# A recurrent scan inside a feed-forward kernel: four stacked copies of the states (high and low part against A's high and low part) in one fp32r product of 32 columns per step

## The chip, the cores and the metric

The kernel runs on one core of a Trainium2 chip. The metric is the device time of one execution in microseconds (us). The engines are named as in the profile: PE (TensorE), DVE (VectorE), ACT (ScalarE), POOL (GpSimd) and SP (SyncE, which issues transfers). They run side by side and meet at semaphores; each works through its own list in order.

## The reference, cut to what matters

```python
x = x + 0.5 * ffn(layernorm(x))                 # front FFN, weights ternary
xB = einsum('bsd,dn->sbn', layernorm(x), B)     # B is 128 x 16
def step(h, xb_t):                              # 512 steps in order, 8 sequences, 16 states
    h = tanh(xb_t + h @ A.T)
    return (h, h)
_, hs = scan(step, 0, xB)
x = x + einsum('sbn,nd->bsd', hs, C) @ W_out.T + b_out
x = x + 0.5 * ffn(layernorm(x))                 # the same FFN again
# ffn: silu(x w1) * (x w2), gelu(. h1), gelu(. h2), . w3 ; widths 128, 512, 512, 512, 128
```

x is 8 x 512 x 128, all of it float32.

## The kernel before

**Tiles and turns.** The 4096 tokens are cut into 8 chunks of 512 columns. The FFN runs over each chunk twice, so there are 16 turns (g = 0 to 15), each of some 25 us. A turn of the PE program is layer 2 of g (four output tiles m, four k each), the first layer of g+1 (`layer1`, four m), layer 3 of g (four m) and layer 4 of g, interleaved. Every product is two fp32r matmuls of 512 columns (`y_hi`, then `y_lo`, both against `w_hi`, L243), because activations are kept as a high part and a rest. ACT makes tanh and gelu (L933, L951, L954), DVE and POOL make the products of the gate and the rests `y_lo` (L659, L669, L676, L686, L1162).

**The scan.** The 512 steps of a sequence are cut into 8 blocks of 64, all blocks at once. A first pass runs chunks 3 to 7 of every block from zero, a full pass of 8 chunks then starts from the ends that the first one found. That is 13 chunk passes of 8 steps. The first four are in the early turns g = 2 to 5 (`early_turn`), the fifth and one of the full pass in g = 6, one each in g = 7 and 8 (`middle_turn`), and the last five in g = 9 to 13 (`turn`). Turns 0, 1, 14 and 15 hold no step. At the end the starts and the ends are compared for equality of every value, and only where they differ does another round run.

**A step before.** States lie on 128 partitions (8 sequences x 16 states) and a step has 8 columns (the blocks). PE multiplies by `a_blk`, A eight times on the diagonal, in float32 (L375), on top of the inputs that one product with `ident` put into the bank `SC` (L371, once for a chunk); ACT takes the tanh into `h_all` (L970). PE's next step waits for ACT's `step_h`.

**Around it.** `x_times_b` (L359) makes the inputs for all sequences, `own_xb` on DVE picks each one's own (L728, L732). `spread_states` on DVE (L713) writes the states of a chunk to 512 columns, each sequence's rows kept by a mask, and `attention` (L381) multiplies that by C W_out in float32; DVE adds it to x as `lnin` (L721). `front_tokens` and `to_features("f", ...)` are the transposes (L262, L272) on both sides of the layer norm that feeds `layer1` of the next turn: DVE takes statistics and normalises (L619, L624, L647), POOL makes the inverse root (L1154, L1157), ACT copies `xn_hi` (L928), DVE makes `xn_lo` (L654). `middle_tokens` (L252) does the same for the norm ahead of the scan.

The order on every engine is the order in which its program is written. There is no scheduler.

## Time and profile before

| | us |
|---|---|
| median of three runs (lowest, highest) | 430.62 (430.44, 431.69) |
| the profiled execution, its own time | 430.41 |
| its span, from the first to the last instruction | 428.6 |
| PE busy | 401.9 (94%) |
| PE weight loads busy | 315.5 (74%) |
| DVE busy | 323.7 (76%) |
| ACT busy | 233.8 (55%) |
| POOL busy | 165.0 (38%) |

A matmul's time in the profile holds its way through the array, and the next one starts long before it ends. So what a matmul costs is read from the distance of two starts. Granted clock of PE over the span: 0.988, and 1.00 in every stretch of 30 us from 30 to 390.

### The profile page before, as it was taken

The numbers are of one execution on the slowest core, as the hardware profiler recorded it, in microseconds if no ns is written. First come the engines' busy times: TensorE is split into PE (matmuls) and PEld (weight loads), VectorE is DVE, ScalarE is ACT, GpSimd is POOL, SyncE is SP. The second block draws the span as 40 slices with busy tenths as digits, with TensorE's granted clock in tenths as the row PEclk, the third lists the DMA queues.
The fourth block names the chain that finished last, engine by engine and source line by source line (L and its number), as shares of the span: only waits on it lengthen the run. The fifth ranks groups of instructions, "written<-read, shape, count | busy, mean of one in ns | idle before, by whom it ended". The sixth has DMA issues, their size and how long they took to land.

```text
span 428.6 us, 6790 instructions
## 1 busy us (share of the span) xinstructions
PE 401.9 (94%) x1917; PEld 315.5 (74%) x1917; DVE 323.7 (76%) x686; ACT 233.8 (55%) x466; POOL 165.0 (38%) x150
## 2 busy tenths in 40 slices
PE   5978999999999999999999999999999999999981
PEld 3756777878878787887777878787877878777660
DVE  4768898998989899569767686949678695978511
ACT  3656464664646466454565546466464656646450
POOL 3435253454514345323434332435343343534120
PEclk9899999999999999999999999999999999999996
DMA  8900000000000000001001010000101000010001
GB/s 260 419 10 2 25 2 17 11 0 26 1 25 0 17 7 0 26 0 50 1 1 51 0 50 0 26 25 2 49 0 49 0 24 24 0 50 1 26 1 33
DMA packets 6079, 14.03 MB, mean 33 GB/s; under 512 B 1056, under 2 KB 1568, under 8 KB 5792
## 3 DMA queue, kind: packets, MB, share of 16 engines
q1 hardware_dynamic: 5040, 13.37, 8.2%
q10 hardware_dynamic: 1008, 0.29, 0.3%
q8 instruction: 14, 0.23, 0.2%
q14 instruction: 17, 0.14, 0.1%
HBM read 7.37 MB, written 2.10 MB: 22 GB/s over the span
## 4 chain that ended last, share of the span: by engine, by line
PE 60%; DVE 16%; issue 11%; ACT 6%; POOL 3%; DMA 1%; DVEq 0%; ACTq 0%; POOLq 0%
PE F L243 47%; PE FR L243 5%; DVE y L669 3%; DVE y_lo L686 3%; DVE u L659 3%; DVE h_wide L713 2%; ACT y_hi L954 2%; PE SC L375 2%; DVE y_hi L676 2%; POOL y_lo L1162 2%; PE MI L381 2%; DVE xnt_f L647 1%; PE MI L252 1%; ACT y L951 1%; ACT th L933 1%
## 5 line engine op out<-in xcount | busy, mean ns | idle before, releaser
L243 PE MATMUL F<-y_hi,w_hi 128*128 128x512 f32 x512 | 214.6, 419 | 8.9 <-DVE y_lo L686 5.0
L243 PE MATMUL F<-y_lo,w_hi 128*128 128x512 f32 x512 | 202.0, 394 | 0.0
L1162 POOL TENSOR_TENSOR y_lo<-y,y_hi 128x512 fp32r<-128x512 f32 x96 | 133.2, 1401 | 129.5 <-ACT y_hi L954 63.7
L951 ACT ACTIVATE y<-F,sc 128x512 f32<-128x512 f32 x112 | 77.1, 688 | 121.6 <-PE F L243 121.5
L243 PEld LDWEIGHTS F<-y_hi,w_hi 128*128 128x128 f32 x512 | 96.4, 188 | 35.7 <-issue 11.4
L243 PEld LDWEIGHTS F<-y_lo,w_hi 128*128 128x128 f32 x512 | 96.5, 189 | 19.7 <-issue 1.9
L686 DVE TENSOR_TENSOR y_lo<-y,y_hi 128x512 fp32r<-128x512 f32 x96 | 83.8, 883 | 33.7 <-ACT y_hi L954 32.4
L954 ACT ACTIVATE y_hi<-F,sc 128x512 fp32r<-128x512 f32 x112 | 76.7, 684 | 0.0
L933 ACT ACTIVATE th<-F,s1h 128x512 f32<-128x512 f32 x61 | 42.2, 691 | 22.2 <-PE F L243 19.2
L243 PE MATMUL F<-xn_hi,w_hi 128*128 128x512 f32 x119 | 50.1, 421 | 3.0 <-POOL w_lo L1202 1.7
L243 PE MATMUL F<-xn_lo,w_hi 128*128 128x512 f32 x119 | 46.9, 394 | 0.0
L669 DVE SCALAR_TENSOR_TENSOR y<-F,s12h,u 128x512 f32<-128x512 f32 x58 | 43.5, 749 | 3.9 <-DVE u L659 0.3
L659 DVE SCALAR_TENSOR_TENSOR u<-th,F 128x512 f32<-128x512 f32 x61 | 41.6, 681 | 6.3 <-ACT th L933 6.0
L375 PEld LDWEIGHTS SC<-h_all,a_blk 128*128 128x128 f32 x208 | 38.1, 189 | 8.1
L676 DVE CAST y_hi<-y 128x512 fp32r<-128x512 f32 x60 | 34.8, 579 | 2.1
L970 ACT ACTIVATE h_all<-SC 128x8 f32 (+1 forms) x104 | 18.3, 176 | 27.4 <-PE SC L375 27.4
L375 PE MATMUL SC<-h_all,a_blk 128*128 (+1 forms) x208 | 30.1, 217 | 0.0
L243 PEld LDWEIGHTS F<-xn_hi,w_hi 128*128 128x128 f32 x119 | 22.4, 188 | 9.0 <-issue 4.0
L1154 POOL TENSOR_TENSOR ve_f<-mv_f,epsc 128x4 f32<-128x4 f32 x16 | 3.2, 200 | 66.7 <-DVE mv_f L624 61.8
L243 PE MATMUL FR<-y_hi,w_hi 128*128 128x512 f32 x64 | 26.3, 412 | 0.6 <-DVE y L669 0.6
L243 PE MATMUL FR<-y_lo,w_hi 128*128 128x512 f32 x64 | 25.2, 394 | 0.0
L243 PEld LDWEIGHTS F<-xn_lo,w_hi 128*128 128x128 f32 x119 | 22.5, 189 | 3.5
(113 smaller groups left out, 341.5 us busy)
## 6 DMA issues: line engine op xcount, KB each, us to landing
x_all<-in_xT SPq DMA_DIRECT2D x1, 2048.0 KB, 16.2
x_all<-x1c SPq DMA_DIRECT2D x8, 256.0 KB, 2.4
x_all<-lnin SPq DMA_DIRECT2D x8, 256.0 KB, 2.3
out<-outb SPq DMA_DIRECT2D x8, 256.0 KB, 2.0
x_all<-in_xtok SPq DMA_DIRECT2D x1, 1536.0 KB, 12.1
w_raw<-in_h1T SPq DMA_DIRECT2D x2, 512.0 KB, 7.9
w_raw<-in_h2T SPq DMA_DIRECT2D x2, 512.0 KB, 9.7
x_all<-in_xtok SPq DMA_DIRECT2D x2, 256.0 KB, 4.8
```

The costliest lines, as they stand in the source:

```text
L243: mm = nc.tensor.matmul(out, wtile(w, layer, k, m), y, start=first and i == 0, stop=last and i == len(pairs) - 1)
L375: nc.tensor.matmul(SC[:, t * BLOCKS:(t + 1) * BLOCKS], a_blk[:, :], h_all[:, bass.ds(off, BLOCKS)], start=False, stop=t == CSTEPS - 1, ski ...
L381: mm = nc.tensor.matmul(MI[:, :], cw_rep[:, :], h_wide[:, :, :].rearrange("p b s -> p (b s)"), start=True, stop=True)
L659: nc.vector.scalar_tensor_tensor(out=u[:, m % 2, :], in0=th[:, m % 2, :], scalar=1.0, in1=l1_banks(g, m, late)[0][:, :], op0=ALU.add, op1= ...
L669: nc.vector.scalar_tensor_tensor(out=y1[:, m, :], in0=l1_banks(g, m, late)[1][:, :], scalar=s12h[:, m:m + 1], in1=u[:, m % 2, :], op0=ALU. ...
L676: nc.vector.tensor_copy(y1_hi[:, m, :], y1[:, m, :]).then_inc(y1_hi_r, 1)
L686: nc.vector.tensor_tensor(y_lo[:, k, :], y[:, k, :], y_hi[:, k, :].bitcast(F32), ALU.subtract).then_inc(out_sem, 1)
L933: nc.scalar.activation(th[:, m % 2, :], l1_banks(g, m, late)[0][:, :], ACT.Tanh, scale=s1h[:, m:m + 1]).then_inc(th_r, 1)
L951: nc.scalar.activation(y23[:, m, :], bankt[:, :], ACT.Gelu, scale=s)
L954: nc.scalar.activation(y_hi[:, m, :], bankt[:, :], ACT.Gelu, scale=s).then_inc(hi_r, 1)
L970: nc.scalar.activation(h_all[:, bass.ds(c * HCOLS + (t + 1) * BLOCKS, BLOCKS)], SC[:, t * BLOCKS:(t + 1) * BLOCKS], ACT.Tanh).then_inc(ste ...
L1162: pool.tensor_tensor(y_lo[:, k, :], y[:, k, :], y_hi[:, k, :].bitcast(F32), ALU.subtract).then_inc(out_sem, 1)
```

## The change

The states get four copies on the partitions: two halves of the sequences (`HALVES`) by two, and in each 32 rows two sets of 16. A step now has 32 columns (4 sequences x 8 blocks). Rows 0 to 63 of `h` hold the low part of the states and rows 64 to 127 the high part; the columns of `a_mix` hold A's high and low part. One fp32r product of 128 x 128 by 32 columns makes a step. ACT takes the tanh twice (into `h`, and for the lower 64 rows once more, unrounded, back into the unused half of the bank `SC`), and DVE subtracts (`scan_low`) before PE may go on. The inputs are no longer put in by a product with the identity: `x_times_b` writes them straight into `SC` for the first pass, ACT keeps a copy (`keep_xb`), and writes it back for later chunks (`inject`). The own-sequence pick and the spread are gone; `attention` is two fp32r products of 256 columns. At the start DVE makes the mixed weights (`mix_parts`). The orders of the turns change on PE, ACT and DVE.

```diff
             def x_times_b(c):
                 pe.wait_ge(xn2_r, c + 1)
-                for j in range(SEQS // PAIR):
-                    rows = slice(j * PAIR * STATES, (j + 1) * PAIR * STATES)
-                    mm = nc.tensor.matmul(MI[rows, 0:PAIR * HCOLS],
-                                          b_rep[:, :, :].rearrange("p b n -> p (b n)"),
-                                          xn2[:, j * PAIR * HCOLS:(j + 1) * PAIR * HCOLS], start=True, stop=True)
+                wait(pe, step_h, c * CSTEPS)
+                for j in range(2 * HALVES):
+                    half = j % HALVES
+                    mm = nc.tensor.matmul(SC[j * 2 * STATES:(j + 1) * 2 * STATES, 0:HCOLS], b_rep[:, :],
+                                          xn2[:, half * HCOLS:(half + 1) * HCOLS], start=True, stop=True)
                 mm.then_inc(xb_mm, 1)
...
-                    nc.tensor.matmul(SC[:, 0:HCOLS], ident[:, :], cols(xb_all, c, HCOLS), start=True, stop=False,
-                                     skip_group_check=True)
-                wait(pe, step_h, s)
-                off = c * HCOLS + t * BLOCKS
-                nc.tensor.matmul(SC[:, t * BLOCKS:(t + 1) * BLOCKS], a_blk[:, :], h_all[:, bass.ds(off, BLOCKS)],
-                                 start=False, stop=t == CSTEPS - 1, skip_group_check=True).then_inc(step_mm, 1)
+                    pe.wait_ge(sc_set, n + 1)
+                wait(pe, step_h, n * CSTEPS + t)
+                if t == 0:
+                    states = h_first[:, :] if isinstance(c, int) and c == 0 else h[:, span(CSTEPS - 1)]
+                else:
+                    states = h[:, span(t - 1)]
+                nc.tensor.matmul(SC[:, span(t)], a_mix[:, :], states, start=False, stop=True,
+                                 skip_group_check=True).then_inc(step_mm, 1)
             def attention(gb, c):
-                pe.wait_ge(spread, gb + 1)
+                pe.wait_ge(step_h, (gb + FIRST_PASS + 1) * CSTEPS)
                 wait(pe, x2_r, gb)
-                mm = nc.tensor.matmul(MI[:, :], cw_rep[:, :], h_wide[:, :, :].rearrange("p b s -> p (b s)"),
-                                      start=True, stop=True)
+                for half in range(HALVES):
+                    mm = nc.tensor.matmul(MI[:, half * HCOLS:(half + 1) * HCOLS], cw_mix[:, half, :], h[:, :],
+                                          start=True, stop=True)
                 mm.then_inc(att_mm, 1)
...
# ACT
-                nc.scalar.activation(h_all[:, bass.ds(c * HCOLS + (t + 1) * BLOCKS, BLOCKS)],
-                                     SC[:, t * BLOCKS:(t + 1) * BLOCKS], ACT.Tanh).then_inc(step_h, 1)
+                nc.scalar.activation(h[:, span(t)], SC[:, span(t)], ACT.Tanh)
+                nc.scalar.activation(SC[0:64, span(CSTEPS + t)], SC[0:64, span(t)], ACT.Tanh).then_inc(step_t, 1)
+            def keep_xb(c):
+                act.wait_ge(xb_mm, c + 1)
+                place = (c + FIRST) % CHUNKS if isinstance(c, int) else c + FIRST
+                nc.scalar.copy(cols(xb_all, place, HCOLS), SC[:, 0:HCOLS]).then_inc(sc_set, 1)
+            def inject(n, c):
+                act.wait_ge(step_h, n * CSTEPS)
+                nc.scalar.copy(SC[:, 0:HCOLS], cols(xb_all, c, HCOLS)).then_inc(sc_set, 1)
...
# DVE
+            def scan_low(n, t):
+                dve.wait_ge(step_t, n * CSTEPS + t + 1)
+                nc.vector.tensor_tensor(h[0:64, span(t)], SC[0:64, span(CSTEPS + t)], h[0:64, span(t)].bitcast(F32),
+                                        ALU.subtract).then_inc(step_h, 1)
...
+            def mix_parts():
+                dve.wait_ge(parts, 1)
+                dve.wait_ge(cw_ready, 2)
+                for i, raw in enumerate((a_raw, cw_rep)):
+                    nc.vector.tensor_tensor(part_lo[:, i, :], raw[:, :], part_hi[:, i, :].bitcast(F32), ALU.subtract).then_inc(parts, 1)
+                dve.wait_ge(ld_scan, 48)
+                for i in range(3):
+                    nc.vector.tensor_scalar(part_own[:, i, :], part_hi[:, min(i, 1), :].bitcast(F32), mask[:, 2 * i:2 * i + 1], None,
+                                            ALU.mult).then_inc(parts, 1)
+                dve.wait_ge(parts, 6)
+                for i, out in enumerate((a_mix[:, :], cw_mix[:, 0, :], cw_mix[:, 1, :])):
+                    nc.vector.scalar_tensor_tensor(out=out, in0=part_lo[:, min(i, 1), :], scalar=mask[:, 2 * i + 1:2 * i + 2],
+                                                   in1=part_own[:, i, :], op0=ALU.mult, op1=ALU.add).then_inc(mixed, 1)
```

The orders of the turns move at many places; three of them follow as the built programs have them.

DVE, early turn g = 2 (before, from the statistics of the middle norm, `st_m`, to the first product of the gate, `u`):

```order
L619 BN_STATS st_m<-MI 128x6 x4
L622 MEMSET spare 128x1
L624 BN_AGGR mv_m<-st_m 128x2 x4
L619 BN_STATS st_f<-x_all 128x6 x4
L622 MEMSET spare 128x1
L624 BN_AGGR mv_f<-st_f 128x2 x4
L647 TENSOR_SCALAR xnt_m<-MI,mv_m,rs_m 128x128 x4
L647 TENSOR_SCALAR xnt_f<-x_all,mv_f,rs_f 128x128 x4
L686 TENSOR_TENSOR y_lo<-y,y_hi 128x512 x2
L659 SCALAR_TENSOR_TENSOR u<-th,F 128x512
```

The same place after the change, from step 1's subtraction on (`h<-SC,h` is `scan_low`):

```order
L721 TENSOR_TENSOR h<-SC,h 64x32
L658 TENSOR_SCALAR xnt_m<-MI,mv_m,rs_m 128x128 x4
L658 TENSOR_SCALAR xnt_f<-x_all,mv_f,rs_f 128x128 x4
L721 TENSOR_TENSOR h<-SC,h 64x32
L697 TENSOR_TENSOR y_lo<-y,y_hi 128x512
L721 TENSOR_TENSOR h<-SC,h 64x32
L697 TENSOR_TENSOR y_lo<-y,y_hi 128x512
L670 SCALAR_TENSOR_TENSOR u<-th,F 128x512
L721 TENSOR_TENSOR h<-SC,h 64x32
L680 SCALAR_TENSOR_TENSOR y<-F,s12h,u 128x512
```

Eight such subtractions stand in the turn; that of step 2 stands behind both normalisations, that of step 4 between the gate's two products.

DVE, the loop of late turns g = 10 to 13, after the change (before, the same rows without L721, and with the statistics first):

```order
L721 TENSOR_TENSOR h<-SC,h 64x32
L647 REGISTER_ALU
L630 BN_STATS st_f<-FR 128x6 x4
L632 REGISTER_ALU
L633 MEMSET spare 128x1
L635 BN_AGGR mv_f<-st_f 128x2 x4
L720 REGISTER_ALU
L721 TENSOR_TENSOR h<-SC,h 64x32
L54 REGISTER_ALU
L658 TENSOR_SCALAR xnt_f<-FR,mv_f,rs_f 128x128 x4
L720 REGISTER_ALU
L721 TENSOR_TENSOR h<-SC,h 64x32
```

Step 0's subtraction stands ahead of the statistics, step 1's ahead of the normalisation and step 2's behind it. On PE, in `turn`, step 0 now stands ahead of layer 2's first tile, step t behind its tile t-1, and `front_tokens` inside the first tile:

```diff
-                if not last:
-                    front_tokens(g + 1)
-                layer2(g, 0, gen)
                 step(0)
+                layer2(g, 0, gen, lambda k: front_tokens(g + 1) if k == 1 and not last else None)
+                step(1)
                 layer2(g, 1, gen)
-                step(1)
+                step(2)
                 layer2(g, 2, gen)
-                step(2)
+                step(3)
                 if not last:
                     to_features("f", xnt_f, FR, g + 1)
                 layer2(g, 3, gen)
-                step(3)
+                step(4)
```

ACT, early turn g = 2, after the change, from the tanh of step 5 on (L1046 and L1047 are a step's two tanh, L1009 the gate's, L1027 and L1030 a gelu's two):

```order
L1046 ACTIVATE h<-SC 128x32
L1047 ACTIVATE SC<-SC 64x32
L1009 ACTIVATE th<-F,s1h 128x512
L1027 ACTIVATE y<-F,sc 128x512
L1030 ACTIVATE y_hi<-F,sc 128x512
L1046 ACTIVATE h<-SC 128x32
L1047 ACTIVATE SC<-SC 64x32
L1027 ACTIVATE y<-FR,sc 128x512
```

Each step's pair stands one gelu earlier than before, so ACT waits there for a PE step that is issued behind the tile whose gelu comes next.

## Rows read from the trace of the kernel before

**Rows 1.** The page, part 1.

```profile
PE 401.9 (94%) x1917; PEld 315.5 (74%) x1917; DVE 323.7 (76%) x686; ACT 233.8 (55%) x466; POOL 165.0 (38%) x150
```

**Rows 2.** Timeline of PE, a step between two tiles: start, us, instruction.

```profile
135.37 0.28 PE L375 MATMUL SC<-h_all,a_blk 128*128 x2
135.51 0.47 PE L243 MATMUL F<-xn_hi,w_hi 128*128 128x512 f32 x1
135.82 0.39 PE L243 MATMUL F<-xn_lo,w_hi 128*128 128x512 f32 x1
136.05 0.40 PE L243 MATMUL F<-xn_hi,w_hi 128*128 128x512 f32 x1
```

**Rows 3.** Timeline of ACT, the tanh of the step in rows 2.

```profile
135.78 0.18 ACT L970 ACTIVATE h_all<-SC 128x8 f32 x1 [1.07 <-PE SC L375]
```

**Rows 4.** Groups by line and shape: count, busy us, mean ns.

```profile
L713 DVE TENSOR_TENSOR h_wide<-h_all,mask 128x512 f32<-128x512 f32 x8 | 14.2, 1779 | 0.0
...
L624 DVE BATCH_NORM_AGGREGATE mv_f<-st_f 128x2 f32<-128x6 f32 x64 | 6.0, 156 | 0.7
```

**Rows 5.** Timeline of PE, x_times_b in an early turn.

```profile
143.23 0.39 PE L243 MATMUL F<-y_lo,w_hi 128*128 128x512 f32 x1
143.55 0.43 PE L359 MATMUL MI<-xn,b_rep 128*32 128x128 f32 x8
143.91 0.66 PE L272 MATMUL FR<-ident,xnt_f 128*128 128x128 f32 x4
```

**Rows 6.** Timeline of DVE, early turn g = 4.

```profile
124.95 0.89 DVE L619 BATCH_NORM_STATS2 st_m<-MI 128x6 f32<-128x128 f32 x4 [0.98 <-PE MI L252]
...
129.12 3.08 DVE L647 TENSOR_SCALAR xnt_f<-x_all,mv_f,rs_f 128x128 f32 x4
...
133.44 0.69 DVE L659 SCALAR_TENSOR_TENSOR u<-th,F 128x512 f32<-128x512 f32 x1
...
145.38 1.29 DVE L686 TENSOR_TENSOR y_lo<-y,y_hi 128x512 fp32r<-128x512 f32 x2
```

**Rows 7.** Timeline of PE, early turn g = 4.

```profile
121.95 0.49 PE L243 MATMUL F<-y_hi,w_hi 128*128 128x512 f32 x1
...
130.79 0.28 PE L375 MATMUL SC<-h_all,a_blk 128*128 x2
...
131.32 0.48 PE L243 MATMUL F<-xn_hi,w_hi 128*128 128x512 f32 x1
...
146.21 0.47 PE L243 MATMUL F<-y_hi,w_hi 128*128 128x512 f32 x1 [0.26 <-DVE y_lo L686]
```

**Rows 8.** Timeline of DVE, late turn g = 11.

```profile
303.58 0.88 DVE L619 BATCH_NORM_STATS2 st_f<-FR 128x6 f32<-128x128 f32 x4
...
306.45 1.37 DVE L647 TENSOR_SCALAR xnt_f<-FR,mv_f,rs_f 128x128 f32<-128x128 f32 x4 [1.57 <-POOL rs_f L1157]
```

**Rows 9.** Timeline of ACT, late turn g = 11.

```profile
308.61 0.69 ACT L951 ACTIVATE y<-F,sc 128x512 f32<-128x512 f32 x1 [0.74 <-PE F L243]
...
309.82 0.60 ACT L928 CAST xn_hi<-FR 128x512 fp32r<-128x512 f32 x1
```

**Rows 10.** Timeline of PE, late turn g = 11.

```profile
311.37 0.49 PE L243 MATMUL F<-xn_hi,w_hi 128*128 128x512 f32 x1 [0.28 <-DVE xn_lo L654]
...
323.30 0.39 PE L243 MATMUL F<-y_lo,w_hi 128*128 128x512 f32 x1
323.79 1.12 PE L381 MATMUL MI<-h_wide,cw_rep 128*128 128x512 f32 x2
...
324.99 0.40 PE L243 MATMUL F<-y_lo,w_hi 128*128 128x512 f32 x1
```

**Rows 11.** Timeline of DVE, end of late turn g = 11.

```profile
325.02 0.69 DVE L686 TENSOR_TENSOR y_lo<-y,y_hi 128x512 fp32r<-128x512 f32 x1
```

**Rows 12.** Timeline of DVE at the start.

```profile
27.66 0.15 DVE L857 TENSOR_SCALAR general<-F 1x1 int32<-1x1 f32 x1 [1.59 <-PE F L606]
```

**Rows 13.** Windows, turn g = 11: length, busy us (records) by engine, clock, DMA.

```profile
303.94:329.11 25.17, 24.79 (x117) 19.62 (x116) 19.27 (x36) 13.78 (x29) 9.46 (x8) 1.00 0.05 21
```

More of the change, by code:

```diff
@@ L741, in early_turn, with step @@
+            def early_turn(g, mid, scan):
+                def step(t):
+                    if scan is not None:
+                        scan_low(scan, t)
                 xn_low(g + 1)
+                step(0)
                 if mid is not None:
@@ L747, in early_turn @@
                 normalise("f", g + 2, cols(xt_all, g + 2), mv_f, rs_f, xnt_f)
+                step(2)
                 low(g, 1, y2_hi_r, y23, y2_hi, y2_lo, y2_lo_dve)
+                step(3)
                 low(g, 3, y2_hi_r, y23, y2_hi, y2_lo, y2_lo_dve)
[L750 to L751 removed]
+                gate(g + 1, 0)
+                step(4)
+                gated(g + 1, 0)
+                gate(g + 1, 1)
+                y1_high(g + 1, 0)
+                gated(g + 1, 1)
+                step(5)
+                y1_high(g + 1, 1)
+                layer1(g + 1, 2)
+                step(6)
                 low(g, 1, y3_hi_r, y23, y3_hi, y3_lo, y3_lo_dve)
+                step(7)
                 low(g, 2, y3_hi_r, y23, y3_hi, y3_lo, y3_lo_dve)
```

309 lines of the change are left out of this document (179 added, 130 removed).

## The prediction

> **What bounds the kernel now.** I read the page first: PE is busy for 94% of the span, the others for 76% and less [rows 1]. Then the timelines of PE, DVE and ACT over one early turn, one late turn and the start. PE's list is nearly gapless; two matmuls of 512 columns start 0.23 us apart [rows 2]. In the early turn g = 4 (some 25 us from the first product of layer 2 at 121.95) PE waits at one place that the rows name, layer 4's last k at 146.21, for a rest that DVE makes [rows 7]. But DVE is close behind: from the statistics at 124.95 it works almost without a pause to that rest at 145.38, through a normalisation of 3.08 us that is slow because POOL works beside it [rows 6]. In the late turn g = 11 (25.17 us [rows 13]) PE waits before `layer1` for `xn_lo` [rows 10], which hangs on ACT's list (gelu, gelu, then `xn_hi` at 309.82 [rows 9]), and before attention for the spread. So the kernel is bound by PE with two chains through ACT and DVE hard beside it. What PE saves counts only outside these chains.
>
> **What PE saves.** A step between two matmuls: 135.82 - 135.37 - 0.23 = 0.22 us [rows 2], for two weight loads and two tiny products (x2 in the row of one step). One fp32r product is one of each: 0.11 saved, 104 x 0.11 = 11.4 us. The identity product is of the same kind: 13 x 0.22 = 2.9. Attention: 324.99 - 323.30 - 2 x 0.23 = 1.22 us, of it a wait of 0.26 (323.79 against 323.53) [rows 10]; the work of 0.96 becomes 512 columns in two pieces, 0.25, so 0.7 saved and the wait gone, at most 8 x 0.97 = 7.8. `x_times_b` costs 143.91 - 143.23 - 0.23 = 0.45 [rows 5], and its columns double: between 0 and 0.45 more; I take 0.2, since its four products write different rows and eight records lie within 0.43 us: 8 x 0.2 = 1.6 lost. Together 20.5 us if no one else set the pace.
>
> The Trainium skill (TensorE: Matmul & The Clock Gate, section on LDWEIGHTS) gives a load as its columns over 1.2 GHz, an estimate of 107 ns for 128. The trace agrees (0.22 for two), and by that rule alone the steps would give back 104 x 0.107 = 11.1 us.
>
> **What a step's result now waits for.** Before: ACT's tanh starts 0.41 us after the step's first product, 0.30 after its second [rows 2, 3]. Afterwards PE may go on when the first tanh, the second, and DVE's subtraction are done. A small operation on DVE takes 0.16 us [rows 4]; I take 0.10 to 0.16 of DVE's list and 0.15 until PE starts. That alone is some 0.8 us, and steps are 2 us apart in early and late turns. What matters is where the subtraction stands on DVE, whose list is in order.
>
> The Trainium skill (VectorE: DVE Perf Modes, section on the TRN2 errata) says that each small operation pays a fixed cost; its PSUM form, 120 cycles plus the elements, gives an estimate of 0.16 us for 32 elements, 16.5 us of DVE's time for 104. The row agrees for the single one. By that rule the turns where DVE is full get longer whatever PE saves, which is the direction of my forecast.
>
> **Early turns (g = 2 to 5).** Times from the turn's first product. Step 2's subtraction stands behind both normalisations. They end at 129.12 + 3.08 - 121.95 = 10.25 [rows 6, 7]; PE's pieces ahead of the statistics (one step, the identity) shrink by 0.33, so 9.9. The subtraction ends at 10.0, PE's step 3 may start at 10.15. Before it started at 130.79 - 121.95 = 8.84 [rows 7], and PE would now be there at 8.3: a wait of 1.8 us. `layer1` starts at 10.15 + 0.4 (the transposes; 131.32 - 130.79 is 0.53 with the old step) = 10.55, before 9.37 [rows 7]: 1.2 later. Queued on ACT behind the tanh of step 3 is the last gelu of layer 2, then the gate's tanh. From there DVE's chain (gate at 133.44 to the rest at 145.38: 11.9 us [rows 6]) gets four subtractions, the first of which sits between the gate's two products and waits for a step that PE issues after `layer1`: +0.2 to 0.7 in all. PE gets 0.44 back from four steps, and `x_times_b` lies in the wait before layer 4. DVE's chain decides: 1.2 + 0.3 - 0.4 (gelus and rests whose waits for ACT fall away as layer 3 comes with less queued) = 1.1 us longer, between 0.3 and 2.0. Four turns: +4.4. `own_xb` goes, 0.9 us at the end of DVE's turn, but the next statistics wait for PE's transposes, not for DVE (idle 0.98 us before them [rows 6]).
>
> **Late turns (g = 9 to 13).** Take the end of layer 3 (323.30 [rows 10]) as 0. DVE's last rest starts at 1.72 (325.02 [rows 11]) whatever attention costs, and layer 4's last k needs it: 2.47. With attention short PE waits there for 0.5, so of attention's 0.97 only 0.4 is real. Step 1 waits for the subtraction of step 0 behind layer 4's output (0.25). The statistics start at about 5.6, the normalisation ends 306.45 + 1.37 - 303.58 = 4.24 later [rows 8], 9.85, and step 2's subtraction behind it; PE's step 3, there at 9.8, starts at 10.15. ACT now takes the tanh of step 3 ahead of the third gelu: 10.15 + 0.3, and that gelu at 10.6. From a gelu's start to `layer1` it is 311.37 - 308.61 = 2.76, less 0.06 for a tanh that moved [rows 9, 10]: 13.3. Before, it was 311.37 - 323.30 + 25.17 = 13.24 [rows 10, 13]. So everything that PE saved in the first half is gone; the second half keeps four steps, 0.44. I take 0.35 saved a turn, between 0 and 0.9: five turns, -1.75.
>
> **Middle turns (g = 6 to 8).** In g = 6 sixteen steps stand 4 matmuls apart (0.94 + 0.11 = 1.05 us) with the 0.8 us above and DVE's and ACT's other work between; a few waits of 0.4 eat the 1.8 us saved by steps, and `x_times_b` now waits for the last of eight of them: 0. In g = 7 and 8 the spread of 1.78 us [rows 4] is off the path to attention, attention stands inside layer 4, and waits in the steps take the rest: -0.5 each, -1.0.
>
> **Start.** `mix_parts`, eight operations of 128 columns, stands ahead of the flag `general`, on which PE's branch waits, and DVE has 1.59 us idle there [rows 12]. At 0.16 to 0.4 us each, and two turns through semaphores, they take 2.3 us: +0.7, between 0 and 1.8.
>
> Sum: 0.7 + 4.4 + 0 - 1.0 - 1.75 = +2.35 us. Against the profiled execution's own 430.41 that is 432.8; the median of the runs is 0.2 above it: 433.0.
>
> **The rivals.**
> 1. Forecast, slightly slower (431.9 to 437), chance 0.46: the subtraction behind the normalisations holds PE in the early turns.
> 2. PE's savings come through (418 to 429.3), chance 0.28. Mechanism: the early normalisation is faster or ends earlier (it takes 3.08 us only because of POOL; at the 1.37 of the late one [rows 8] step 3 would be held for 0.1 to 0.5, not 1.8), and the early turns gain 0.5 each instead of losing 1.1: -6.4 against my sum, 426.5. It decides the sign from 0.6 us less wait in each early turn on (2.35 / 4), and from 0.9 on it can be measured. With all chains slack it would be 430.6 - 20.5 + 0.7 = 411, against which rows 6 and 10 speak.
> 3. The terms cancel (429.3 to 431.9), chance 0.19: early turns +0.5, late -0.35.
> 4. Waits feed on one another (437 to 445), chance 0.05: each of 104 steps adds 0.1 on a DVE that is full in four turns and close to it in nine, 430.6 + 10 = 441.
> 5. The scan's ends differ in their last bits and a second round runs: eight turns, some 430 + 200 = 630. Chance 0.02: inputs are sums over 128 normalised values, tanh is mostly saturated, and both start and end are kept to a high and a low part, so nothing speaks for fewer agreeing bits.
>
> **How the numbers follow.** Likeliest 433.0. Its own range from the bounds: early 1.2 to 8, late 0 to -4.5, start 0 to 1.8, middle -2.5 to 1, gives 430 to 437. Case 2 has its middle at 426; to leave out no more than 2 in 10 the range is 425 to 438. A measurement of this kernel tells about 0.3%, 1.3 us, from no change. Faster 0.28, same 0.2, slower 0.52.
>
> **What would show it.** Right: in turns g = 2 to 5 PE idles 1 to 2 us before step 3, released by DVE's subtraction, and these turns last 26 us and more; late turns last 24.6 to 25.0, with a wait before `layer1` of 0.4 or more; a lone step costs PE 0.11. Wrong: early turns of 24.5 or less (rival 2), the subtraction over 0.3 us (rival 4), or a wait of ACT, not DVE, in front of the steps.

## The result and the profile after

The changed kernel takes 432.53 us (median of 5 runs, 432.42 to 433.62) against 430.62 before (median of five runs): a ratio of 1.0037 with a 95% interval of 1.0024 to 1.005, slower by a little more than the 0.3% that the prediction took as the least that tells. Measured once more beside the experiments below, the ratio was 1.0051 (1.0034 to 1.0068). The profiled execution has a span of 430.7 us, 2.1 more than before. One execution of the kernel before, beside the later runs, took 849.09 us; nothing here explains it, and the ratios leave it out.

Page of the changed kernel, busy time by engine, and two groups of its costliest instructions (line, engine, operation, tiles, count, then busy us and mean ns of one, then idle time before them):

```profile
PE 391.6 (91%) x1787; PEld 298.0 (69%) x1787; DVE 323.5 (75%) x774; ACT 248.4 (58%) x585; POOL 165.5 (38%) x150
...
L389 PEld LDWEIGHTS SC<-h,a_mix 128*128 128x128 f32 x103 | 19.3, 187 | 18.9 <-DVE h L721 14.2
L721 DVE TENSOR_TENSOR h<-SC,h 64x32 fp32r<-64x32 f32 x104 | 18.2, 175 | 13.2 <-ACT SC L1047 12.3
```

PE's busy share fell from 94% [rows 1] to 91%, and the time did not fall with it: the work saved became waiting. The waits of PE in the changed kernel (engine and line that waited, engine and line waited for, us in total, times, longest):

```profile
PE F L256 <- DVE y_lo L697: 8.0, 12, 1.8
PE SC L389 <- DVE h L721: 6.9, 8, 1.6
PE FR L284 <- DVE xnt_f L658: 2.5, 2, 2.1
```

The second row is new. It is a scan step (L389) that waits for DVE's subtraction of the step before (L721); it stands in one place of each of the four early turns, 1.33 us in g = 2 and 1.6 in the others (6.1 of the 6.9 us). Timeline of PE, early turn g = 5, which begins at 150.60 (start us, duration, line, operation, and in brackets the idle time and what ended it):

```profile
156.91 0.18 PE L389 MATMUL SC<-h,a_mix 128*128 128x32 f32 x1
...
158.67 0.40 PE L256 MATMUL F<-y_lo,w_hi 128*128 128x512 f32 x1
160.66 0.28 PE L389 MATMUL SC<-h,a_mix 128*128 128x32 f32 x1 [1.60 <-DVE h L721]
160.79 0.66 PE L284 MATMUL MI<-ident,xnt_m 128*128 128x128 f32 x4
161.21 0.48 PE L256 MATMUL F<-xn_hi,w_hi 128*128 128x512 f32 x1
```

Step 3 starts 10.06 us after the turn's first product and `layer1` 10.61 after it; before, in g = 4, they stood at 8.84 and 9.37 [rows 7]. The same stretch of DVE and POOL:

```profile
156.14 1.37 DVE L658 TENSOR_SCALAR xnt_m<-MI,mv_m,rs_m 128x128 f32<-128x128 f32 x4 [0.33 <-POOL rs_m L1258]
157.43 3.09 DVE L658 TENSOR_SCALAR xnt_f<-x_all,mv_f,rs_f 128x128 f32 x4
160.44 0.17 DVE L721 TENSOR_TENSOR h<-SC,h 64x32 fp32r<-64x32 f32 x1
```
```profile
157.32 2.60 POOL L1263 TENSOR_TENSOR y_lo<-y,y_hi 128x512 fp32r<-128x512 f32 x2
```

The subtraction takes 0.17 us, but it comes behind a normalisation of 3.09, during most of which POOL makes two rests.

Lengths of the turns, from the first product of layer 2 in one turn to that in the next, taken from the starts in each trace (us):

| turn | before | after | difference |
|---|---|---|---|
| g = 1 begins at | 48.74 | 49.66 | +0.92 |
| g = 2 to 5 | 24.70, 25.09, 25.07, 24.80 | 25.42, 26.06, 26.04, 25.81 | +3.67 |
| g = 6 | 27.47 | 26.94 | -0.53 |
| g = 7 and 8 | 26.21, 26.21 | 25.92, 25.91 | -0.59 |
| g = 9 to 13 | 25.06, 25.23, 25.17, 25.17, 24.99 | 24.33, 24.93, 24.63, 24.69, 24.16 | -2.88 |
| g = 14 | 23.07 | 23.96 | +0.89 |

Some 0.35 us of the gain of g = 6 and of the loss of g = 14 only moved over a border: `front_tokens` (four transposes) stood ahead of a turn's first product and now stands behind its second k (the second of a tile's four parts). The last output of layer 4 is written at 421.63 instead of 420.12, 1.5 us later; the remaining 0.6 of the span lies behind it (8.5 us before, 9.1 after), and in a second profile of the kernel before that stretch was 9.6 and in one of the changed kernel 8.4, so it is spread and not the change. From the start to the last output the differences of the table add up to 1.5 us.

### The profile page after: what moved, and what is told of

Its sections match the earlier page's. It is cut to its first block, busy times and chain, and to the rows that moved or that the text cites. A ratio compares the mean times of both kernels' runs of the same rounds, so it can differ in the third digit from the quotient of the medians.

```text
span 430.7 us, 6662 instructions
## 1 busy us (share of the span) xinstructions
PE 391.6 (91%) x1787; PEld 298.0 (69%) x1787; DVE 323.5 (75%) x774; ACT 248.4 (58%) x585; POOL 165.5 (38%) x150
## 4 chain that ended last, share of the span: by engine, by line
PE 49%; issue 20%; DVE 14%; POOL 7%; ACT 7%; DMA 1%; ACTq 0%; DVEq 0%; POOLq 0%
PE F L256 39%; PE FR L256 4%; POOL y_lo L1263 4%; ACT y_hi L1030 3%; DVE y_lo L697 3%; DVE u L670 2%; DVE xnt_f L658 2%; DVE y L680 2%; POOL rs_m L1258 1%; PE FR L284 1%; PE SC L389 1%; DVE xnt_m L658 1%; DVE st_m L630 1%; ACT y L1027 1%; PE SC L374 1%
## 5 line engine op out<-in xcount | busy, mean ns | idle before, releaser
L697 DVE TENSOR_TENSOR y_lo<-y,y_hi 128x512 fp32r<-128x512 f32 x96 | 87.2, 914 | 42.9 <-ACT y_hi L1030 42.2
L1027 ACT ACTIVATE y<-F,sc 128x512 f32<-128x512 f32 x112 | 76.6, 684 | 53.6 <-PE F L256 53.5
L1030 ACT ACTIVATE y_hi<-F,sc 128x512 fp32r<-128x512 f32 x112 | 76.4, 682 | 0.0
L1046 ACT ACTIVATE h<-SC 128x32 fp32r<-128x32 f32 x104 | 20.4, 197 | 83.0 <-PE SC L389 82.4
L1009 ACT ACTIVATE th<-F,s1h 128x512 f32<-128x512 f32 x61 | 41.9, 687 | 20.3 <-PE F L256 17.8
L687 DVE CAST y_hi<-y 128x512 fp32r<-128x512 f32 x60 | 38.0, 633 | 1.1
L389 PEld LDWEIGHTS SC<-h,a_mix 128*128 128x128 f32 x103 | 19.3, 187 | 18.9 <-DVE h L721 14.2
L721 DVE TENSOR_TENSOR h<-SC,h 64x32 fp32r<-64x32 f32 x104 | 18.2, 175 | 13.2 <-ACT SC L1047 12.3
L389 PE MATMUL SC<-h,a_mix 128*128 128x32 f32 x103 | 20.6, 200 | 6.9 <-DVE h L721 6.9
```

Source lines behind the costliest of these rows:

```text
L389: nc.tensor.matmul(SC[:, span(t)], a_mix[:, :], states, start=False, stop=True, skip_group_check=True).then_inc(step_mm, 1)
L687: nc.vector.tensor_copy(y1_hi[:, m, :], y1[:, m, :]).then_inc(y1_hi_r, 1)
L697: nc.vector.tensor_tensor(y_lo[:, k, :], y[:, k, :], y_hi[:, k, :].bitcast(F32), ALU.subtract).then_inc(out_sem, 1)
L721: nc.vector.tensor_tensor(h[0:64, span(t)], SC[0:64, span(CSTEPS + t)], h[0:64, span(t)].bitcast(F32), ALU.subtract).then_inc(step_h, 1)
L1009: nc.scalar.activation(th[:, m % 2, :], l1_banks(g, m, late)[0][:, :], ACT.Tanh, scale=s1h[:, m:m + 1]).then_inc(th_r, 1)
L1027: nc.scalar.activation(y23[:, m, :], bankt[:, :], ACT.Gelu, scale=s)
```

## The experiments

All edits are made to the changed kernel. Ratios are to the kernel before, measured on the same chip; 1% is 4.3 us. The changed kernel itself stands at 1.0037 and 1.0051.

### 1. The early subtraction between the two normalisations

```diff
 # DVE, early_turn
                     normalise("m", mid, MI, mv_m, rs_m, xnt_m)
+                step(2)
                 normalise("f", g + 2, cols(xt_all, g + 2), mv_f, rs_f, xnt_f)
-                step(2)
```

> One edit against the changed kernel: in the early turns DVE's subtraction of step 2 goes between the two normalisations instead of behind both. My theory (the subtraction's place holds PE's step 3): in g = 5 the second tanh of step 2 ends at 157.24 + 0.18 = 157.42 and the first normalisation at 157.5, so the subtraction costs its 0.1 to 0.2 us and waits for nothing; step 3 on PE goes from 10.06 us after the turn's first product to 8.3, its wait of 1.60 us goes, and the four early turns, 25.4 to 26.1 now, last 24.6 to 25.1: about -4.0 us, 428.5. Rival A (the subtraction's own time on a full DVE is what counts, not its place): under 1 us, 431.6 to 432.5, with the wait turned up elsewhere in the same turn, before layer 3 or layer 4. Rival B (the second normalisation, later by one subtraction, holds the transposes of the next tile): a wait before them and 430 to 431.

Measured: 426.01 us, ratio 0.9872 (0.9846 to 0.9898), 6.5 us less than the changed kernel. The turns g = 2 to 5 last 23.82, 24.29, 24.31 and 24.06, 6.85 less together. Timeline of DVE and PE in its turn g = 4, which begins at 121.59:

```profile
127.14 1.37 DVE L658 TENSOR_SCALAR xnt_m<-MI,mv_m,rs_m 128x128 f32<-128x128 f32 x4 [0.34 <-POOL rs_m L1258]
...
128.46 0.18 DVE L721 TENSOR_TENSOR h<-SC,h 64x32 fp32r<-64x32 f32 x1
128.56 2.97 DVE L658 TENSOR_SCALAR xnt_f<-x_all,mv_f,rs_f 128x128 f32 x4
```
```profile
129.90 0.18 PE L389 MATMUL SC<-h,a_mix 128*128 128x32 f32 x1
```

The subtraction has no idle time in front of it, the normalisation is nearly as long as it was (2.97 us), and step 3 comes 8.31 us after the turn's first product with no wait. So the place of one operation of 0.18 us in DVE's list cost 1.6 to 1.8 us in each of four turns. That is more than I expected (about 4.0): I had thought that DVE's chain behind the gates would hold the turn at its old length, and it does not; the turns are now 0.7 to 0.9 shorter than before the change, close to the 0.9 that PE saves in them (eight steps of 0.11 and the identity product, less 0.2 for `x_times_b`). Both rivals fall.

### 2. The late subtraction ahead of the normalisation

```diff
 # DVE, turn
                 step(1)
+                step(2)
                 if not last:
                     normalise("f", g + 1, FR, mv_f, rs_f, xnt_f)
-                step(2)
```

> One edit against the changed kernel: in the late turns DVE's subtraction of step 2 goes ahead of the normalisation. In g = 11 the second tanh of step 2 ends at about 309.4 and the normalisation starts at 309.35, so it is pushed back by 0.1 to 0.2 us. My theory: PE's step 3 stops waiting (0.3 us a turn), the third gelu comes 0.3 earlier, and xn_hi and layer 1 with it: 0.2 to 0.3 in each of five turns and the one without a scan untouched, -1.2 us, 431.3. Rival (layer 1 hangs on the normalisation through the transposes of the next tile, not on the scan): step 3 comes earlier, but the transposes 0.15 later, and the time stays within 0.4 us or grows.

Measured: 432.92 us, ratio 1.0036 (1.002 to 1.0052). The turns g = 9 to 13 last 24.24, 24.63, 24.53, 24.55 and 24.06, 0.73 less together. The wait at step 3 (0.34 us of its weight load in g = 11) is gone, but there PE now waits 0.48 us for `xn_lo` before `layer1`, 0.33 in the changed kernel:

```profile
314.93 0.49 PE L256 MATMUL F<-xn_hi,w_hi 128*128 128x512 f32 x1 [0.48 <-DVE xn_lo L665]
```

About half of what I expected, and too little to see in the time. The rival describes it better: what holds `layer1` is mostly not the scan.

### 3 and 4. The start: ACT's cast later, and `mix_parts` later

```diff
 # ACT, at the start (3 and 4)
             hi_part(2)
-            act.wait_ge(ld_scan, 48)
-            nc.scalar.copy(part_hi[:, 0, :], a_raw[:, :]).then_inc(parts, 1)
...
             hi_part(3)
+            act.wait_ge(ld_scan, 48)
+            nc.scalar.copy(part_hi[:, 0, :], a_raw[:, :]).then_inc(parts, 1)
             y1_high(0, 0)
 # DVE, at the start (4 alone)
-            mix_parts()
             dve.wait_ge(gen_mm, 1)
...
             first_stats(2)
+            mix_parts()
             normalise("f", 2, cols(xt_all, 2), mv_f, rs_f, xnt_f)
```

> One edit against the changed kernel: ACT's cast of the recurrence matrix, with its wait for the last of three small transfers, goes from ahead of the first gate's tanh to behind the fourth piece of the weights, where ACT is idle for 0.60 us. The first gate's tanh started at 13.96 us before and starts at 14.62 in the changed kernel. My theory (this wait made two thirds of the start's loss, not the eight operations of mix_parts): the turn g = 1 starts 0.66 us earlier, at 49.0, and the time falls by 0.66, to 431.9. Rival (mix_parts ahead of the flag is the whole loss, as forecast): no change at g = 1 and in the time, since the flag waits for them either way.

> The edit of the run before it, and mix_parts moved on DVE from ahead of the flag to between the statistics and the normalisation of tile 2, where DVE is idle for 1.40 us (its eight operations take 1.9 us, and 0.95 us more are idle after the next rest). Theory: both parts of the start's loss go, 0.66 + 0.25, the turn g = 1 starts at 48.75 as in the kernel before, and the time is 0.9 us below the changed kernel's: 431.6. Rival (mix_parts is the whole loss): the two edits together give the same 0.9, but the one before gives none of it. Second rival (the gap is too short and the rest behind it comes late): no more than the first edit alone.

Measured: 432.86 us, ratio 1.0045 (1.003 to 1.0061), and 432.55, 1.0029 (1.0014 to 1.0043). The turn g = 1 begins at 49.84 and 49.99, not at 49.0 and 48.75. With the cast out of the way the first gate's tanh starts no earlier than in the changed kernel's profile (14.62), because it waits for PE:

```profile
14.79 0.69 ACT L1009 ACTIVATE th<-F,s1h 128x512 f32<-128x512 f32 x1 [3.15 <-PE MI L256]
```

But this profile can't test the theory. PE's granted clock was 0.50 here for 6.8 us from 9.72 on, so PE was late; in two other profiles with such a stretch (experiments 2 and 6) the tanh starts at 14.77 with the cast still in its way. Where the clock stayed at 1.00 in these microseconds, ACT's cast is what the tanh follows. ACT in the kernel of experiment 1:

```profile
13.62 0.30 ACT L1181 CAST part_hi<-a_raw 128x128 fp32r<-128x128 f32 x1 [1.94 <-DMA mask<-in_mask]
13.82 0.68 ACT L1009 ACTIVATE th<-F,s1h 128x512 f32<-128x512 f32 x1
```

In the second profile of the kernel before, which has no cast and the same clock there, this tanh starts at 13.07, released by PE. Layer 1 on PE starts 0.07 us later in experiment 1's kernel (10.91 and 10.84), the tanh 0.75. So the wait for the transfer costs some 0.7 us where PE is fast, and is hidden where PE is slow; three of the ten profiles of changed kernels with the cast in its old place show the tanh right behind it. Over twelve runs the third kernel is not faster than the changed one, so a gain on average is not shown.

`mix_parts` is the smaller thing that I took it for: in the changed kernel the flag comes 1.99 us after the reduction ahead of it (26.58 to 28.57), in the fourth run 1.74 (26.72 to 28.46), as before (1.75): it costs 0.25. Its DVE rows in the changed kernel, eight operations in 1.9 us, of which 1.6 fill an idle time [rows 12]:

```profile
26.58 0.16 DVE L927 TENSOR_REDUCE ne_sum<-ne_cnt 128x1 f32<-128x7 f32 x1
26.66 0.29 DVE L743 TENSOR_TENSOR part_lo<-a_raw,part_hi 128x128 f32<-128x128 f32 x1
...
28.57 0.14 DVE L930 TENSOR_SCALAR general<-F 1x1 int32<-1x1 f32 x1
```

What the fourth run saved there it gave back at once: the normalisation that follows took 3.18 us, beside two of POOL's subtractions instead of one, where it had taken 2.08. What else moves the start is the matter of experiment 9.

### 5. The states' high part alone

```diff
 # ACT, scan_step
-                nc.scalar.activation(h[:, span(t)], SC[:, span(t)], ACT.Tanh)
-                nc.scalar.activation(SC[0:64, span(CSTEPS + t)], SC[0:64, span(t)], ACT.Tanh).then_inc(step_t, 1)
+                nc.scalar.activation(h[64:P, span(t)], SC[64:P, span(t)], ACT.Tanh).then_inc(step_h, 1)
 # DVE, scan_low: nothing is left of it; at the start all of h is set to zero
```

> Against the changed kernel: the states' low part is left out. ACT writes one tanh a step, to the rows of the high part alone (the rows of the low part stay zero), and tells PE itself that the step is done; the second tanh and DVE's subtraction are not there, so the states are kept to fp32r alone. My theory (DVE's answer and its place in its list is what holds PE): PE waits for ACT alone, the early turns lose their 1.6 to 1.8 us as they did when the subtraction of step 2 was moved (24.0 to 24.3 us each), the last of eight steps no longer holds x_times_b in g = 6 (0.84 us), the steps there no longer wait (0.2), and the late turns lose 0.2 to 0.4: together 7 + 1.2 + 1.5, about 423. Rival A (it is only the one place in the early turns): 425.5 to 426. Rival B (the product of 32 columns and its place on PE and ACT hold the steps, not DVE): over 428. If the ends of the scan then differ in their last bits a second round runs, and the time is some 630.

Measured: 422.27 us, ratio 0.9779 (0.9762 to 0.9796), within 1 us of my 423; rivals A and B fall. The early turns last 23.83 to 24.24, g = 6 is 1.14 shorter, g = 7 and 8 are 0.7 each, g = 9 to 13 0.75 together. So the low part of the states costs the changed kernel some 10 us; seven of them are experiment 1, and two and a half stand in the middle turns, where steps are 1.05 us apart. The edit takes out ACT's second tanh (0.18 us a step) as well as DVE's subtraction, so it does not divide these two and a half between the engines, and no run here tried another order in the middle turns. One expectation missed: before `x_times_b` in g = 6 PE still waits 0.73 us, now for ACT, instead of 0.84.

### 6. The subtraction twice

```diff
 # DVE, scan_low
+                nc.vector.tensor_tensor(h_twice[0:64, :], SC[0:64, span(CSTEPS + t)], h[0:64, span(t)].bitcast(F32),
+                                        ALU.subtract)
                 nc.vector.tensor_tensor(h[0:64, span(t)], SC[0:64, span(CSTEPS + t)], h[0:64, span(t)].bitcast(F32),
                                         ALU.subtract).then_inc(step_h, 1)
```

> Against the changed kernel: DVE does each step's subtraction twice, the first time into a spare tile, so that its list has 104 more operations of the disputed kind and each step's answer comes one such operation later. My theory (a single subtraction costs only where PE is waiting for DVE): about 0.1 us for each of the nine turns with a wait at step 3, the same at x_times_b and the two waits of g = 6, 0.1 to 0.2 a turn more from DVE's chain behind the gates: +1.2 to +2.5 us, 434 to 435. Rival (my forecast's case 4: DVE's list is full, each operation is paid in full): 104 x 0.10 to 0.17, +10 to +17 us, 443 to 450.

Measured: 436.58 us, ratio 1.0115 (1.0101 to 1.013), 4.0 us more than the changed kernel's first median and 3.2 more than its second, over my bound (2.5) and far under the rival's. Two groups of DVE in it:

```profile
L722 DVE TENSOR_TENSOR h_twice<-SC,h 64x32 fp32r<-64x32 f32 x104 | 18.2, 175 | 14.2 <-ACT SC L1050 13.2
L724 DVE TENSOR_TENSOR h<-SC,h 64x32 fp32r<-64x32 f32 x104 | 17.8, 171 | 0.0
```

104 more operations, which start 0.10 us apart, make 10 us of DVE's list and cost 0.1 to 0.35 in most turns. The excess has another cause. Turns g = 2 and 3 are 0.2 longer, but g = 4 and 5 are 1.67 and 1.74 longer. Timeline of PE in g = 4, and three windows of this turn (window, length, busy us and records of each engine, granted clock, DMA share, GB/s):

```profile
135.28 0.28 PE L390 MATMUL SC<-h,a_mix 128*128 128x32 f32 x1 [1.73 <-DVE h L724]
...
136.27 0.63 PE L257 MATMUL F<-xn_lo,w_hi 128*128 128x512 f32 x1
136.69 0.63 PE L257 MATMUL F<-xn_hi,w_hi 128*128 128x512 f32 x1
```
```profile
125.15:135.00 9.85, 8.40 (x39) 6.64 (x39) 8.38 (x33) 4.29 (x12) 4.91 (x6) 1.00 0.07 27
136.00:139.00 3.00, 3.00 (x9) 2.36 (x8) 1.19 (x4) 1.71 (x3) 0.00 (x0) 0.50 0.00 0
139.81:152.86 13.05, 12.88 (x64) 9.23 (x62) 11.72 (x23) 8.67 (x22) 5.72 (x4) 1.00 0.00 0
```

Some 0.7 us behind the end of the wait of 1.73 us the granted clock falls to 0.50 for 3.4 us, 1.2 instead of 2.4 GHz; matmuls start 0.43 us apart instead of 0.23, and the turn loses 1.5 us. The waits at step 3 in this kernel are 1.49, 1.72, 1.73 and 1.72 us in g = 2 to 5; the clock fell behind the last two. After the waits of the changed kernel (1.33 and three of 1.6) it stayed at 1.00 in all of these turns. Without the two stretches the profiled execution would be 2.2 us over that of the changed kernel (435.9 - 430.7 - 3.0), inside my bound. The Trainium skill (TensorE: Matmul & The Clock Gate, section on HAM oscillation) says that waits between groups of matmuls can put the array back to half rate and that the work behind them then starts cold; this trace agrees for two of three waits of 1.72 us, and the third shows that the same wait need not do it.

### 7. POOL's rests behind the normalisation

```diff
 # POOL, early_turn
                 inverse_std("f", g + 2, mv_f, ve_f, rs_f)
+                if mid is not None:
+                    pool.wait_ge(normed["f"], g + 3)
                 rest(g, True)
```

> One edit against the changed kernel: in the early turns from g = 1 on POOL starts its two rests of layer 2 only when DVE's normalisation of the next tile is done; they took 2.60 us from 157.32 on, beside that normalisation (157.43, 3.09 us for four operations), and layer 3 needs them at about 165. Theory (POOL's work beside it is what makes the normalisation slow; my forecast's case 2 turned on this): it takes 2.1 us, as the same operations do at 32.51 us where POOL is idle, the subtraction behind it comes 1.0 earlier, PE's wait at step 3 falls from 1.60 to 0.6 and the four early turns shorten by 0.8 to 1.0 each: 428.5 to 429.5, unless the two rests then come late for layer 3 (a wait of PE for POOL at layer 3's first or third k). At 1.4 us (the length of the late turns' normalisation, from PSUM) the wait would vanish and the time be 426. Rival (the operations are slow by themselves, from SBUF in fp32): 3.0 us as before and no change, 432.5.

Measured: 427.19 us, ratio 0.9905 (0.9888 to 0.9922), 5.3 us less than the changed kernel with the order of experiment 1 untouched. Timeline of DVE and POOL in its turn g = 5, and the wait of PE there:

```profile
155.44 1.11 DVE L658 TENSOR_SCALAR xnt_f<-x_all,mv_f,rs_f 128x128 f32 x4
156.46 0.17 DVE L721 TENSOR_TENSOR h<-SC,h 64x32 fp32r<-64x32 f32 x1
...
156.77 2.86 POOL L1263 TENSOR_TENSOR y_lo<-y,y_hi 128x512 fp32r<-128x512 f32 x2 [1.41 <-ACT y_hi L1030]
```
```profile
161.74 0.50 PE L256 MATMUL F<-xn_hi,w_hi 128*128 128x512 f32 x1 [0.30 <-DVE y L680]
```

The same four operations take 1.11 us instead of 3.09. I had expected 2.1, from a row at 32.51 where I took POOL to be idle; it makes one rest there (1.29 us from 32.44). So there are three lengths: 1.11 with none of POOL's subtractions beside the normalisation, 2.08 with one, 3.0 to 3.1 with two. Step 3 waits no more, and the early turns last 24.02 to 24.68. That they are 0.2 to 0.4 us longer than in experiment 1 fits the wait in the last row: DVE's next rest, now beside POOL's, took 1.56 us instead of 0.69. The Trainium skill (SBUF — State Buffer, section on the two separate sides) says that DVE and GpSimd share one pair of ports as a lock that is held for a whole instruction, not as a split of bandwidth. The trace agrees as far as it goes: in the changed kernel the one from SBUF is 2.0 us longer in the time in which POOL does two operations of 1.3. The normalisation from PSUM (`xnt_m`) takes 1.37 us with 0.2 us of a POOL subtraction beside it (at 156.14) and 1.37 with 1.2 us of one (at 181.91).

### 8. `xn_hi` ahead of the third gelu

```diff
 # ACT, turn (with the edit of experiment 2 on DVE)
                 step(3)
+                if nxt:
+                    front(g + 1)
                 gelu2(g, 2)
-                if nxt:
-                    front(g + 1)
                 step(4)
```

> Two edits against the changed kernel, both in the late turns: DVE's subtraction of step 2 ahead of the normalisation (as in an earlier run, which took 0.1 to 0.3 off each turn), and on ACT xn_hi ahead of the third gelu of layer 2. In that earlier run, g = 11: the transposes end at about 312.4, ACT runs the third gelu's two passes from 312.24 and xn_hi only at 313.39, xn_lo follows at 314.01 and layer 1 starts 9.46 us after the turn's first product, where PE would have been ready at 8.85. Theory (layer 1 hangs on ACT's order, gelu before xn_hi): xn_hi comes 0.9 us earlier, layer 1 starts at 8.85, each of the five turns with a scan loses 0.4 to 0.6 and the one without a little: 2.0 to 3.0 us below the changed kernel's time beside the 0.7 of the first edit: 429 to 430. Rival (the gate's chain, with the third and fourth gelu 1.2 us later on ACT, then ends later and layer 4 waits longer for its last rest): layer 1 starts earlier, but the turns stay within 0.2 us, 431.5 to 432.5.

Measured: 430.02 us, ratio 0.9967 (0.9954 to 0.998), at the upper end of what I expected. The turns g = 9 to 13 last 23.96, 24.24, 24.12, 24.15 and 23.65. Timeline of ACT and PE in g = 11, which begins at 303.95:

```profile
311.18 0.59 ACT L1004 CAST xn_hi<-FR 128x512 fp32r<-128x512 f32 x1 [0.35 <-PE FR L284]
311.66 0.69 ACT L1027 ACTIVATE y<-F,sc 128x512 f32<-128x512 f32 x1
...
312.78 0.47 PE L256 MATMUL F<-xn_hi,w_hi 128*128 128x512 f32 x1
```

`layer1` starts 8.83 us after the turn's first product, with no wait, against 9.59 in the changed kernel, and 1.9 of the 2.6 us in these turns come from this edit. The gates' chain was not short: the rival falls. What stays is a wait of 0.54 for DVE's rest before layer 4's last k, in g = 11 at 327.06.

### 9. The changed kernel and the one before once more, for the start

> The changed kernel itself, unedited, on the chip of the runs beside it, so that ratios of one chip can be set against it, and for the start: in the profiles of six kernels with the same first 12 us the turn g = 1 began between 49.66 and 51.42 us, while the kernel before began it at 48.74. Theory (the start's difference is made by TensorE's granted clock, which sat at half speed for a different stretch of the first 50 us in each profile, and only 0.25 us of it by mix_parts): g = 1 begins anywhere from 49.0 to 51.5 here, with the clock's windows to match, and the turns from g = 2 on have the lengths of the first profile within 0.05. Rival (the changed start costs a fixed 0.9 us): 49.66 again within 0.1. Ratio to the kernel before 1.002 to 1.005.

> The kernel before, unedited, for one more profile of its start. Theory (the clock makes the start's spread): g = 1 may begin anywhere from 48.5 to 50.5, since this kernel too has its stretches of half clock there. Rival (the changed start costs a fixed 0.9): 48.74 within 0.1. Its turns from g = 1 on keep their lengths within 0.05.

Measured: 433.34 us for the changed kernel, ratio 1.0051; 430.58 in one run for the one before. The turn g = 1 begins at 51.01 and at 47.84; all turns from g = 1 on repeat their lengths within 0.1. So the start has no fixed cost of 0.9. Over all profiles g = 1 begins at 47.84 and 48.74 in the kernel before and between 49.66 and 51.46 in the changed kernel and its edited versions, and the clock goes with it. Windows of PE's granted clock (the last three figures of a row are clock, DMA share, GB/s), the changed kernel's second profile and then the same of the kernel before:

```profile
25.00:30.00 5.00, 2.69 (x12) 1.89 (x12) 4.89 (x17) 1.19 (x3) 0.59 (x1) 1.00 0.00 2
31.00:35.00 4.00, 4.00 (x12) 3.13 (x11) 2.60 (x9) 4.00 (x7) 2.87 (x4) 0.57 0.00 0
```
```profile
10.00:30.00 20.00, 14.96 (x64) 11.03 (x65) 15.59 (x44) 11.63 (x20) 7.98 (x9) 1.00 0.59 244
30.00:50.00 20.00, 18.22 (x79) 13.60 (x78) 15.86 (x24) 11.68 (x21) 9.52 (x7) 1.00 0.00 0
```

There are two stretches at half clock. The first lies between 8 and 17 us, where PE has waited for its first data; it is 0 to 7 us long, and both kernels can have it (0 and 3.4 us in the two profiles of the kernel before). The second is only the changed kernel's. PE waits behind the flag for a rest that DVE makes, the work that `mix_parts` delays, and that wait is 1.52 and 1.53 us in the two profiles of the kernel before and 1.76 to 1.78 in those of the changed kernel and its edited versions:

```profile
30.19 0.47 PE L256 MATMUL F<-y_hi,w_hi 128*128 128x512 f32 x1 [1.77 <-DVE y_lo L697]
```
```profile
28.24 0.47 PE L243 MATMUL F<-y_hi,w_hi 128*128 128x512 f32 x1 [1.52 <-DVE y_lo L686]
```

Of eleven profiles with the longer wait seven show half clock for 3.4 us from 29 to 32 us on (the first profile of the changed kernel is one of the other four); of three with the shorter one (twice the kernel before, and experiment 4) none does. What such a stretch costs can be read off the turn's start, because the rest is steady: from the end of this wait to g = 1 it is 19.59 to 19.62 us in the four profiles with the longer wait that lack it, 19.59 and 19.60 in the two of the kernel before, and 20.81 to 20.83 in the seven that have it: 1.2 us. In the same way the time from the first gate's tanh to the flag is 13.7 in both profiles of the kernel before and in experiment 4, and 13.94 to 13.98 in all the others. So the start is the sum of three things: when that tanh starts (13.07 and 13.96 before, 13.82 to 15.22 after, by the first stretch at half clock and ACT's cast), 0.25 for `mix_parts`, and 1.2 in some executions.

The clock that is listed with every run speaks for the last of them, as an estimate: twice the missing part of the mean clock times the span is the time at half clock, and it averages 11.2 us over 51 runs of the kernel before, 12.8 over the twelve of experiment 3 and 11.1 over the twelve of experiment 4, which differs from it by the place of `mix_parts` alone (each average is good to some 0.5). So 0.25 us of operations on DVE may cost the start about 1 us on average (0.25 + 7/11 x 1.2), and this would account for much of the gap between what the turns lose in the trace (0.6 us from g = 1 on) and what the runs measure (1.6 to 2.2). Experiment 4 gained 0.25 at the flag and lost 0.44 by its slow normalisation, and its runs still average 0.6 us less than those of experiment 3 (432.58 and 433.18). That the longer wait is what brings the clock down is not shown, though: three profiles with the shorter one are few.

### 10 and 11. The edits together

The tenth kernel has the edits of experiments 1, 2 and 8, the eleventh that of 7 as well.

> Three edits against the changed kernel together: in the early turns the subtraction of step 2 between the two normalisations, in the late turns the subtraction of step 2 ahead of the normalisation, and xn_hi ahead of the third gelu on ACT. Theory (the two places are waits of different turns and add up): early turns 23.8 to 24.3 us as in the run of the first edit (6.85 us less in all), late turns 24.0 to 24.2 as in the run of the other two (2.6 less): span 421.2 give or take the start's 1 us, time 423, ratio to the kernel before 0.978 to 0.983, the fastest of the versions that compute the whole. Rival (what the early turns gain is given back where the late ones start, since the transfers and rests between them come at other times): 425 or more.

> The kernel of the run before with one more edit: in the early turns POOL starts its two rests of layer 2 only behind DVE's normalisation of the next tile (alone this took that normalisation from 3.09 to 1.11 us and the early turns to 24.0 to 24.7 us). Theory (with the subtraction already ahead of it, the normalisation's length holds nobody; POOL's later rests then slow DVE's work behind it and the second product of the gates comes late, as in the run of that edit alone, where PE waited 0.3 us before the third part of layer 1): early turns 0 to 0.4 us longer than without it, 423 to 424.5. Rival (a faster normalisation is worth something by itself): 422 or less.

Measured: 423.45 us, ratio 0.9811 (0.9791 to 0.9831), and 425.27, ratio 0.9863 (0.9837 to 0.9888). The turns of the tenth are those of experiments 1 and 8, each within 0.05; the edits add up, and this is the fastest kernel here that computes the whole, 1.9% faster than the kernel before. The eleventh is over the 423 to 424.5 that I expected. In it the early turns g = 2 to 5 are 0.35 to 0.40 longer each, and g = 1, which has no scan, by 0.43. So the fast normalisation is worth something only while a scan step hangs on it.

## Why the prediction was right

**The early turns.** The sentence "Step 2's subtraction stands behind both normalisations" gave PE's step 3 at 10.15 and `layer1` at 10.55; they stand at 10.06 and 10.61, the wait is 1.60 us against 1.8, and four turns lost 3.67 us against 4.4. Experiments 1, 5 and 7 show the mechanism from three sides: move the operation, leave it out, or shorten what is ahead of it, and 5.6 to 7.2 us of these four turns go each time. A wrong step is inside: "DVE's chain decides", with 11.9 us from the gate to the rest. It had slack. Once step 3 was free the turns became 0.7 to 0.9 shorter than before the change, not equal. It did not change the forecast's sign, because the wait at step 3 was longer than the slack; it made me set experiment 1 at half its worth.

**The late turns.** Forecast 0.35 us less in each of five, measured 2.88 together, 1.99 with g = 14, where 0.35 only crossed the border and the rest (0.54) is in no step of mine: half of it is there when the transposes of g = 14 start, 6.94 us after the turn's first product instead of 6.32, behind statistics that DVE starts at 2.71 instead of 2.09; why DVE is later there stays open. The mechanism held in part. Step 3 waited in g = 11 for 0.3 us, and `layer1` came 13.2 us after the end of layer 3 of the turn before, 13.3 by the forecast and 13.2 to 13.3 before. But I laid this on the subtraction and on the tanh ahead of the third gelu; experiments 2 and 8 show that the subtraction makes 0.1 to 0.3 and that ACT's old order, gelu before `xn_hi`, makes 0.4 in most turns, as it already did in the kernel before [rows 9].

**The middle turns.** 0 for g = 6 and -0.5 each for g = 7 and 8: measured -0.53, of which 0.35 crossed the border, and -0.3 each. The waits named there are in the trace: 0.84 us for `x_times_b` behind the last of eight steps, 0.2 before two steps.

**The start.** Forecast +0.7, measured +0.92 in the first pair of profiles and +3.17 in the second, so that agreement is luck: `mix_parts`, all that the term held, delays the flag by 0.25. The size that I gave it (2.3 us of work against 1.59 of idle time) was too long, 1.9. The rest is the granted clock and ACT's wait for a transfer, which no term of the sum had.

**Sum and rivals.** The sum was +2.35, the span grew by 2.1. That is closer than the terms deserve: up to the last output the growth was 1.5, the other 0.6 is spread behind it, and the early turns' term was 0.7 too large. What the forecast had right is the sign and its reason; that 433.0 lies within 0.5 of 432.53 is partly luck. Rival 2's condition, an early normalisation that is not slowed by POOL, is experiment 7; it forecast 426.5 for that and 427.19 was measured, so that one duration of 3.08 us [rows 6] was enough to decide between the forecast and this rival; by experiment 1 the operation's place was enough as well. Rival 4, each step paid in full on DVE, falls with experiment 6; rival 3 did not come about, and the scan's ends agreed, so no second round ran (rival 5). PE's gross saving was well sized: a step costs 0.10 to 0.11 us less (from 2.08 between two tiles of layer 2 to 1.98), attention 0.23 in all instead of 1.22 with its wait (325.74 to 325.97), and `x_times_b` 0.21 more, as taken.

## What to carry to other kernels

When a small operation joins the loop between two engines, price its place in the in-order list before its duration: look for the longest instruction that can stand ahead of it, and for the wait that it then makes on the other side. Here 0.17 us of work cost 1.6 in one place and nothing in another, and moving one line turned a kernel 0.4% slower into one 1.3% faster. Then look at what makes the long instruction long, and read the engines beside it: a normalisation of 3.09 us took 1.11 once POOL was idle beside it. And when an edit shows nothing, look at whether the profile could have shown it: experiment 3's could not, because PE was at half clock in the stretch in question.

## What the runs showed of the hardware

- A normalisation of 4 x 128 columns from SBUF on DVE took 1.11 us with POOL idle, 2.06 to 2.16 with one of POOL's subtractions beside it and 2.71 to 3.18 with two; the same from PSUM took 1.37 with or without one.
- A wait of PE between dense stretches was followed by half clock for 3.4 us in some executions and not in others: behind two of three waits of 1.72 us in experiment 6 and seven of eleven of 1.76 to 1.78 at the start, never behind the 1.60 of the early turns (18 waits in six profiles) or the 1.52 and 1.53 at the start (three profiles). Each such stretch cost 1.2 us at the start and 1.5 in an early turn, nearly as much as the wait itself.
- Small subtractions of 64 x 32 from PSUM start 0.10 us apart on DVE when two follow one another, though each is shown as 0.17.
